# The batch loop of a gather stage, written out or run as a loop of the chip

## The reference

```python
x = xattn(x, ctx, mask, ...)     # chunked attention with 8 heads, then a layer norm over the tokens
idx = top_k(pairwise distances of the tokens' first channels, 30)   # 30 nearest of 1024 points, per token
att = softmax(mlp_with_batch_norms(rho, theta, phi of each neighbour))   # one weight per neighbour
agg = einsum('bnkc,bnk->bnc', x.transpose(0, 2, 1)[bidx, idx], att)
return x + agg.transpose(0, 2, 1)
```

## Time and profile before

| | us |
|---|---|
| median of 3 runs (5477.54 to 5483.57) | 5480.29 |
| the profiled execution | 5483.57 |
| its span, first to last instruction | 5481.8 |
| end of `stage_a` and `stage_b`, start of `stage_e` | about 4253 |

### The profile page before, as it was taken

How to read it: one execution, slowest core, us unless ns; L and a number is a source line. 1 busy time by engine, 2 the same in 40 slices (tenths; PEclk the granted TensorE clock), 3 DMA queues, 4 the chain that set the end, 5 groups by cost and what they waited for, 6 DMA issues and landing times. The chain is left out here.

```text
span 5481.8 us, 164547 instructions
## 1 busy us (share of the span) xinstructions
PE 4338.9 (79%) x62610; PEld 2649.4 (48%) x63182; DVE 5238.8 (96%) x7660; ACT 3867.5 (71%) x9296; POOL 2498.2 (46%) x3044
## 2 busy tenths in 40 slices
PE   6787787777777777877778777773295899999999
PEld 2444444444444444444444444442042677777776
DVE  7999999999999999999999999998998899999997
ACT  3777777777777777777777777776433777777776
POOL 3566676666766666666667666664000000000000
PEclk7898898999988999989889889986597899999999
DMA  1010000010000100001000001000000000010010
GB/s 32 17 31 20 17 18 18 17 33 17 18 17 18 33 17 18 17 18 33 17 18 17 18 23 28 17 9 5 0 0 0 27 32 32 28 34 32 28 34 26
DMA packets 135647, 114.36 MB, mean 21 GB/s; under 512 B 105328, under 2 KB 105840, under 8 KB 134640
## 3 DMA queue, kind: packets, MB, share of 16 engines
q1 hardware_dynamic: 134768, 102.73, 6.4%
HBM read 69.16 MB, written 33.55 MB: 19 GB/s over the span
## 5 line engine op out<-in xcount | busy, mean ns | idle before, releaser
L599 ACT ACTIVATE ohT<-oh_ps 128x512 bf16<-128x512 f32 x1920 | 1153.5, 615 | 170.3 <-PE oh_ps L493 142.3
L896 DVE MAX8 vals<-pd_sb 128x8 f32<-128x1024 f32 x1024 | 1209.0, 1225 | 61.4 <-ACT pd_sb L599 44.2
L901 DVE FIND_INDEX8 idx<-vals,pd_sb 128x8 uint16<-128x1024 f32 x1024 | 1257.0, 1232 | 0.0
L514 PEld LDWEIGHTS g_ps<-tparts,ohT 128*128 128x128 bf16 x23040 | 861.6, 98 | 370.2 <-issue 119.4
L514 PE MATMUL g_ps<-tparts,ohT 128*128 128x24 bf16 x23040 | 877.6, 175 | 91.1 <-ACT ohT L599 43.5
L903 DVE MATCH_REPLACE8 pd_sb<-vals,pd_sb 128x1024 f32<-128x1024 f32 x768 | 940.5, 1225 | 0.0
L1912 PEld LDWEIGHTS e_a_ps<-planes,e_oh 120*128 120x128 bf16 x24576 | 684.4, 97 | 270.3 <-issue 170.0
L738 ACT ACTIVATE sS<-s_ps,mx 128x64 f32<-128x64 f32 x2048 | 612.9, 328 | 241.0 <-DVE mx L920 239.4
L1683 ACT COPY e_at<-e_a_ps 128x512 f32<-128x512 f32 x512 | 543.8, 1062 | 304.4 <-PE e_a_ps L1912 298.0
L493 PE MATMUL oh_ps<-bitsT,code 128*128 128x512 bf16 x1348 | 580.5, 435 | 218.5 <-ACT bitsT L756 133.9
L1912 PE MATMUL e_a_ps<-planes,e_oh 120*128 120x32 bf16 x24576 | 699.8, 177 | 58.8 <-DVE e_oh L1840 58.7
(11 more groups left out here) (277 smaller groups left out, 6697.6 us busy)
## 6 DMA issues: line engine op xcount, KB each, us to landing
ctx_s<-in_ctx SPq DMA_DIRECT2D x32, 512.0 KB, 4.4
maskb<-in_mask_Bx1x_ff SPq DMA_DIRECT2D x32, 512.0 KB, 7.0
x_s<-in_x SPq DMA_DIRECT2D x32, 512.0 KB, 5.5
y_spill<-y_s SPq DMA_DIRECT2D x32, 512.0 KB, 3.0
e_y<-y_spill SPq DMA_DIRECT2D x32, 512.0 KB, 3.9
out<-e_o SPq DMA_DIRECT2D x64, 256.0 KB, 2.4
table<-in_ctx SPq DMA_DIRECT2D x96, 4.0 KB, 5.9
pd_sb<-in_shape_constants SPq DMA_DIRECT2D x1, 1024.0 KB, 5.2
```

What stands on the lines that cost most here:

```text
L514: m = nc.tensor.matmul(found_ps[gi % 2][:, k % GK, t, :], ohT[:, k % OHR, bass.ts(t, P)], tparts[:, par, part, :], start=(part == 0), stop ...
L599: return nc.scalar.activation(dst, src, func, scale=scale, bias=bias)
L896: nc.vector.max(vals[:, i, :], pd_sb[:, (t + i) % RING, :]).then_inc(topk_step, 1)
L901: found = nc.vector.max_index(idx16[:, par, t + i, 8 * r:8 * r + 8], vals[:, i, :], work)
```

## The change

`batches` of `stage_e` no longer writes out the 32 batches. It writes out batches 0, 1, 30 and 31 and runs the 28 between them in a loop of the chip with two batches in its body, as `stage_a` does. Inside the loop `b`, `j` and all that is worked out from them (wait values, the offsets of `planes`, `idx_all`, `rstd`, `nmr`, `y_dram` and `out`) are register values. The order of instructions on each engine stays.

```diff
         def batches(eng, emit):
 
-            for b in range(B):
-                emit(b, b // 2, b % 2, b == B - 1, b < B - 2)
+            emit(0, 0, 0, False, True)
+            emit(1, 0, 1, False, True)
+            with eng.Fori(1, B // 2 - 1) as j:
+                emit(j * 2, j, 0, False, True)
+                emit(j * 2 + 1, j, 1, False, True)
+            emit(B - 2, B // 2 - 1, 0, False, False)
+            emit(B - 1, B // 2 - 1, 1, True, False)
```

## The result

| | us |
|---|---|
| before, median of 4 runs | 5479.84 |
| after, median of 4 runs (5556.25 to 5561.41) | 5558.80 |
| ratio after / before, 95% interval | 1.0143 [1.0126, 1.0162] |
| the profiled execution after, its span | 5562.71, 5560.9 |

The loop is slower by 79 us, 1.4%. The forecast was 5524 us, 44 us more than before, with a range to 5556: the direction was right and the size was not.

The account below looks back on a forecast made before the run. The prediction took TensorE to bound the last stage. 13 branches at 3.05 us (40 us) plus 4 us of registers, 44 us on 5483.57, gave 5528; the median lies 3.3 us lower, so 5524 us, range 5500 to 5556.

Parts of the forecast that it names:

- What bounds the stage: Last stage: TensorE sets the end, so each microsecond it loses there is a microsecond of the kernel.
- The pause at the head: TensorE at each of 13 taken branches: 2.8 us idle before the first transposes, net loss 1.65 us.
- one pause per branch: TensorE's last-stage loop: each taken branch brings one issue pause, about 2.8 us, 13 times, some 36 us together.
- The clock: TensorE drops to the 1.2 GHz level behind nearly every branch: 1.1 us each, bounds none and 3.3 us.
- Registers: Register arithmetic in the loop: 0.3 us exposed per branch, plus 0.07 us x 2 x 28 batches, 4 us, at `add`.
- The other engines' branches: Last-stage loop: VectorE's branch takes 3.6 us, ScalarE's about 3.1, SP's 0.3, all hidden by TensorE's own pause.
- The sum again: Last-stage loop: 1.65 + 0.3 + 1.1 = 3.05 us per branch, 13 of them 40 us, plus 4 us of registers: 44 us.
- 75 were named as a sign: Profile after: 13 taken branches of 3.3 to 4.4 us on TensorE's sequencer, 75 us apart.
- A: Rival: branches cost only TensorE's idle time, no clock loss, registers hidden; 16 to 21 us, 5496 to 5502; chance 0.17.
- B: Rival: register arithmetic not hidden in 56 quads, 40 + 22 us and longer clock loss; 5540 to 5580; chance 0.11.
- C: Rival: no difference, branches cost 0.3 us like SP's and are hidden; only 4 us remain, 5484; chance 0.08.
- D: Rival: faster, the held loop avoids waits at 195 instruction fetches; at 0.1 us each 18 us, 5466; chance 0.04.

Follow-up runs that it names:

- e4_slot0: The changed kernel with the head of TensorE's last-stage loop at the start of a block of 256 instructions; 5536.1 us.
- e6_slot_late: The changed kernel with the head of TensorE's last-stage loop 20 instructions before the end of a block of 256; 5579.1 us.
- e7_pause: The kernel before, written out without branches, with TensorE made to wait for a GpSimd operation at the 13 places of the branches; 5524.9 us.
- e2_others_loop: The changed kernel with TensorE's last stage written out and only SP, ScalarE and VectorE running the loop; 5486.4 us.
- e3_one_edge: The changed kernel with the loop as two turns of 14 batches on all engines, so one taken branch, same register arithmetic; 5490.4 us.
- b1_add_later: The kernel before with VectorE's last-stage addition issued behind the one-hot tile of group 1 instead of group 0; 5428.8 us.
- c3_loop_later: The changed kernel with TensorE's backward branch announced, its loop head at a block's start, and VectorE's addition one one-hot tile later; 5468.6 us.
- d3_slot108: The changed kernel with the head of TensorE's last-stage loop at slot 108 of a block, branch not announced; 5552.8 us.
- e1_pe_loop: The changed kernel with only TensorE running the last-stage loop and the other engines' programs written out; 5567.4 us.
- d1_hint_108: The changed kernel with TensorE's backward branch announced and its loop head at slot 108 of a block; 5487.7 us.
- e5_hint: The changed kernel with TensorE's backward branch announced at the top of the loop body; 5491.0 us.
- d2_later_108: The changed kernel with TensorE's backward branch announced, loop head at slot 108, and VectorE's addition one one-hot tile later; 5440.3 us.

## Why the prediction was right or wrong

- **What bounds the stage.** Right. TensorE alone decides there: its loop alone costs all of it, those of the others nothing that can be told.
- **The pause at the head.** Right in kind and nearly in size: 13 pauses, 36 us predicted, 33.1 measured, the branch held for 3.70 us at the median (3.75 taken), the clock of the stretch 0.95, and the 1.02 us behind the branch gone. In one thing the reason was wrong and did no harm: TensorE's body was said to be longer than that of the first stage. The traces have 1636 matmuls in a turn here and over 2240 there (3359 and 4837 instructions); both are many blocks long.
- **The step that failed: one pause per branch.** The prediction counted the fetch of the target and nothing behind it. A taken branch of TensorE costs two fetches one after the other, since the block behind the target is asked for only when the target's instructions run. Here the head lay 82 instructions before a border, too few to cover it: 32.3 us that no term of the sum held. e4_slot0 and e6_slot_late, which move that pause by the head's place alone, show it. The waits of the first stage could not warn: behind the pause of 3.98 us come 8 transposes and then a wait of 1.28 us for ScalarE, so no second pause is put down to issue. Its fetches could: of the 16 KB packets one starts in the 2 us behind the branch at 956.5 and another between 960.5 and 962.5, when TensorE is back.
- **The clock.** Mechanism right, size wrong: 1.1 us per branch predicted, 25.6 / 13 = 2.0 measured, within the bounds given. e7_pause loses 2.2 us per turn without any branch, so it is standing still and not the fetch. But 1.6 of them fall at a pause of 1.02 us that costs no clock in the kernel before: the size of one pause does not tell its price.
- **Registers.** 0.3 us per branch in the open: not found. 0.07 us x 2 per batch, 4 us: e2_others_loop has 2.7 us in the waits, at one place per batch.
- **The other engines' branches.** Predicted 3.6 us of VectorE and 3.1 of ScalarE, hidden; measured 0.2 us. The price was taken from a loop of 643 instructions for one of 201 (ScalarE: 787 for 118). That did no harm here, but it would have in a stage that VectorE bounds.
- **The sum again**, with what was measured, per branch: 2.55 - 1.02 + 2.49 + 2.0 = 6.0 us, 13 of them 78, and 1 to 3 us of registers, for 79. The branches are 81.2 us apart, where 75 were named as a sign (78 by the sum's own 1096 us for 28 batches).
- **The rivals.** A, without loss of clock, is excluded by the clock of 0.95. B had the right height, 5558.8 of 5540 to 5580, by luck: its cause, register arithmetic in 56 quads, is 4 us in e2_others_loop and e3_one_edge takes the rest away with one branch. C holds for SP, VectorE and ScalarE, and for TensorE only in the one untaken branch. D, gain from fewer fetches: nothing speaks for it. b1_add_later runs TensorE without one gap through straight-line code, so crossing a border in sequence costs nothing here.
- Runtime: NRT & Kernel Launch, Instruction fetch mechanics, of the Trainium skill says that a taken branch breaks the sequential prefetch. The traces agree, and the 32.3 us of the second pause show how far that goes: not only the target is late, but the block behind it too.

What stays open: why the clock costs from 1.4 us per turn (c3_loop_later against b1_add_later, 42.3 less 24.4 us of pause, over 13) to 2.9 us (d3_slot108), why it falls at the pause of 1.02 us in e7_pause and not in the kernel before, and why the packet behind the target starts late in all turns of e1_pe_loop. That a branch must wait for a fetch under way fits all seven placements that ran (four places of the head, three of them with the announcement too) and the turns of e6_slot_late and d1_hint_108 one by one, but the request itself is not in a trace, only its packet.

## What to carry to other kernels

A loop whose body is many blocks of 256 instructions long can cost TensorE two fetches at each taken branch, and where TensorE bounds the stage it pays both, with its clock on top. Bodies of 201 instructions and fewer cost 0.2 us here; in the first stage GpSimd's, of 428, has 13 pauses of 2.6 us put down to issue, and VectorE's, of 643, holds its sequencer for 3.1. Between 201 and 428 nothing was measured. Announce the backward branch, and place the head so that both the next border and the last border before the branch are some 150 instructions away. Then the loop was 0.1% slower than the straight line where a wait of 1 us stood behind the branch anyway, and 0.2% slower where nothing covered it. And a bounded wait that repeats in every batch, as the 45 us of the earlier trace rows, is worth more than the shape of the loop: look first at which queue entry stands in front of the tile that the bounding engine waits for.

## What the runs showed of the hardware that was not expected

- After a taken branch of TensorE the block behind the target is fetched only when the engine is back at work: a second pause of 2.49 us, 82 instructions behind the head; of 3.05 us, 20 behind it; of 1.1 us, 148 behind it; none with 256.
- A branch, even an announced one, waits for a sequential fetch under way: held for 2.9 us with 32 instructions between the last border and the branch, 0.70 with 140, 0.36 with 206 (medians). In e6_slot_late, not announced, it is 4.7 to 5.0 us with such a fetch and 3.3 to 3.4 without.
- An announced branch that is not taken is followed by a pause: 2.6 us in e5_hint, 1.7 in d2_later_108, 0.6 in d1_hint_108.
- From entering a block until the next one can run takes about 3.2 to 3.7 us; this is an estimate from d2_later_108, whose border pauses end 3.6 to 4.1 us after the branch and whose head runs 0.4 us after it.
- Loops of 201 and 118 instructions, on VectorE and ScalarE, branch back in 0.2 us.
- A pause of 2.2 us in every second batch costs 2.2 us of clock per turn, of which 0.4 lie behind it and 1.6 at a pause of 1.02 us in the next batch, which costs nothing in 61 of the 62 pauses of the kernel before.
